# Rotary halves and key scaling of each layer's first step written on VectorE instead of GpSimd

## The chip, the cores and the metric

One core of one Trainium2 chip runs the whole program. The time is the device time of one execution in microseconds (us). It is taken from timed runs; one more execution was recorded by the hardware profiler and gives the rows below. The engines are TensorE (PE in the rows; PEld is its weight load), VectorE (DVE), ScalarE (ACT), GpSimd (POOL) and SyncE (SP).

## What is computed

A two-layer model on 16 sequences of 256 tokens, 128 channels: linear attention, a mixture of experts, a retention block, and last a block of two local-attention layers with feed-forward parts. The change lies in the local attention. Cut to what matters:

```
h = shift_token(x)
q, k, v = split(h @ wqkv)                 # 8 heads of 64
q = l2norm(q) * qs;  k = l2norm(k) * ksc
q = q * cos * scale + rotate_half(q) * sin * scale
k = k * cos / scale + rotate_half(k) * sin / scale
o = local_attention(q, k, v)              # windows of 64, one window back
x = x + o @ wo
```

for 2 layers, each followed by a feed-forward part.

## The kernel before

The attention of a layer (`local_layer`, lines 1977 to 2429) walks over 8 chunks of 512 tokens. A chunk is 4 tiles of 128 tokens. Each engine has a program of its own, written out by hand; semaphores alone order the engines against each other. `steps` (line 2012) calls `step` ten times on each engine: in a step a new chunk is projected (`project`), the chunk before it is attended (`attend`) and the one before that is finished (`finish`). The first step of a layer has `project` alone; the second has `project` and `attend`. So each layer begins with one step in which nothing but the projections of its first chunk runs, until two pairs of heads of that same chunk are attended in its last tile.

What one tile t passes through:

- TensorE: `project_qk` for queries, then for keys (line 2128, three matmuls each). The one for queries waits for `v_sb`, the copy of the values of tile t-1, because it takes that bank.
- ScalarE: `squares` (line 2264) of queries and of keys, the squares for the norms.
- VectorE: `rotate` (line 2354) of queries and of keys, which multiplies the bank by cosines and by sines into `R`; then `lengths` (lines 2361 and 2364), the sums of squares.
- TensorE: `project_v` (line 2137), which waits for both rotations because it takes the bank of the keys; ScalarE copies it out (`keep_values`, line 2290).
- GpSimd: `add_halves` (line 2053, two instructions) adds the cosine and sine parts; then in even tiles `next_low` (lines 1664 and 1666) and in odd ones `mix_values` (lines 2075 and 2076); then `scale_keys` (line 2062), which multiplies the keys by their inverse norms `rn`.
- ScalarE: `norms` (lines 2269 and 2272) gives `rn`. It is called one tile later, as the second piece of work of tile t+1, behind `squares` of its queries.
- TensorE: `turn_keys` (line 2149) and `turn_queries` (line 2158) transpose `R` of tile t, within tile t+1.

VectorE also runs `maxima` (line 2377), the score maxima of two heads in four instructions, twice a tile once attention runs, and `reciprocals` (line 2384). In the first step's last tile it runs `rotate`, `maxima` of pair 0, `lengths`, `maxima` of pair 1.

Below, a layer's tiles are counted from 0: tiles 0 to 3 are its first step, tile 4 is the first tile of its second step. `summed` counts added halves, `normed` scaled keys, `rnorm` inverse norms.

Of the kernel before, what the change touches and what calls it, by code (L numbers as in the profile page):

```python
# [11 lines left out]
ALU = mybir.AluOpType  # L12
# [3 lines left out]
P = 128  # L16
# [19 lines left out]
DEPTH, HEADS, DH, WIN = 2, 8, 64, 64  # L36
# [1930 lines left out]
NTILE = CH // P  # L1967
# [9 lines left out]
def local_layer(k, l, shared):  # L1977
# [4 lines left out]
    nc, ps = k.nc, k.ps  # L1982
    with ExitStack() as big:
# [5 lines left out]
        with ExitStack() as ctx:  # L1989
# [50 lines left out]
            @block.gpsimd  # L2040
            def _(pool):

                def next_low(g, par, part):
                    wait_alone(k, pool, hs_hi, 2 * (g + l) + part + 1)
                    shift_low(k, g, l, par, part)
                    wait_alone(k, pool, shifted, 2 * (g + l) + part + 1)

                def add_halves(g, t):
                    n, i = NTILE * g + t, t % 2
                    halves = R[:, i, :, :, :].rearrange("p q c (h z d) -> p q c h z d", z=2, d=DH // 2)  # L2050
                    wait_alone(k, pool, rotated, 2 * n + 2)
                    for z in range(2):
                        nc.gpsimd.tensor_tensor(halves[:, :, 0, :, z, :], halves[:, :, 0, :, z, :],  # L2053
                                                halves[:, :, 1, :, 1 - z, :], ALU.add).then_inc(summed, 1)

                def scale_keys(c, par, t):
                    n, i = NTILE * c + t, t % 2
                    wait_alone(k, pool, summed, 2 * n + 2)
                    wait_alone(k, pool, rnorm, n + 1)
                    x = R[:, i, 1, 0, :].rearrange("p (h d) -> p h d", d=DH)  # L2060
                    scale = rn[:, par, t, HEADS:2 * HEADS].rearrange("p (h o) -> p h o", o=1)
                    nc.gpsimd.tensor_tensor(x, x, scale.to_broadcast([P, HEADS, DH]), ALU.mult).then_inc(normed, 1)  # L2062

                def scale_weights(c, p):
                    wait_alone(k, pool, rden_r, NPAIR * c + p + 1)
                    x = W[:, p % RING, :].rearrange("p (a b) -> p a b", a=4)
                    scale = rden[:, p % RING, :].rearrange("p (a o) -> p a o", o=1)
                    nc.gpsimd.tensor_tensor(x, x, scale.to_broadcast([P, 4, P]), ALU.mult).then_inc(scaled, 1)  # L2068

                def mix_values(c, par, s):  # L2070
                    need(pool, av_mm, NPAIR * (c - 2) + NB * (s + 1))
                    pool.wait_ge(v_sb, NTILE * c + 2 * s + 2)
                    pool.wait_ge(summed, 2 * (NTILE * c + 2 * s + 2))
                    pool.sem_inc(v_seen, 1)
                    nc.gpsimd.tensor_copy(VM[par][0:DH, s, :, :], VA[par][0:DH, 2 * s + 1, :, :]).then_inc(v_mixed, 1)
                    nc.gpsimd.tensor_copy(VM[par][DH:P, s, :, :], VA[par][DH:P, 2 * s, :, :]).then_inc(v_mixed, 1)
                    wait_alone(k, pool, v_mixed, 2 * (SPC * c + s + 1))

                def step(g, par, project, attend, finish):
                    now = (g, par, project, attend, finish)  # L2080
                    for t in range(NTILE):
                        for lag in (8, 7):
                            sc = staged(*now, 2 * t, lag)
                            if sc:
                                scale_weights(sc[0], sc[2])
                        if project:
                            add_halves(g, t)
                            if t % 2:
                                mix_values(g, par, t // 2)
                            else:  # L2090
                                pool.wait_ge(summed, 2 * (NTILE * g + t + 1))
                                next_low(g + 1, 1 - par, t // 2)
                            scale_keys(g, par, t)
                        elif attend:
                            split_part(t // 2, t % 2)

                done = lambda i: 2 * NX + 3 * DEPTH + 2 * l + i + 1

                def split_part(i, part):
                    n = names[1 + i]  # L2100
                    hi, lo = parts[n]
                    if part == 0:
                        pool.wait_ge(w_in, L * 16 * len(names))
                        nc.gpsimd.tensor_scalar(hi[:], w[n][:], 1.0, None, ALU.mult).then_inc(k.w_hi, 1)
                    else:
                        pool.wait_ge(k.w_hi, done(i))
                        nc.gpsimd.tensor_tensor(lo[:], w[n][:], hi[:].bitcast(F32), ALU.subtract).then_inc(k.w_lo, 1)

                steps(pool, step)
                pool.wait_ge(k.w_lo, done(1))  # L2110
                pool.wait_ge(resid, SPC * (G0 + 2))
                for i in range(2):
                    ffn_shift(k, i, here(G0 + i), ffn_shifted)
                pool.wait_ge(ffn_shifted, 2 * (G0 + 2))
# [228 lines left out]
            def _(dve):  # L2343
# [13 lines left out]
                def lengths(g, t):  # L2357
                    n, i = NTILE * g + t, t % 2
                    dve.wait_ge(squared, 2 * n + 2)
                    need(dve, rnorm, n - 1)  # L2360
                    nc.vector.tensor_reduce(sums[:, i, :, 0:1].rearrange("p h o -> p (h o)"),  # L2361
                                            sq[:].rearrange("p q (h d) -> p (q h) d", d=DH), AX.X, ALU.add).then_inc(sums_r, 1)
                    dve.wait_ge(sums_r, n + 1)
                    nc.vector.tensor_reduce(ss[:, i, :], sums[:, i, :, :], AX.X, ALU.max).then_inc(clipped, 1)

                def maxima(c, par, p):
                    b, s = p % NB, p // NB
                    if b == 0:
                        dve.wait_ge(rnorm, NTILE * c + 2 * s + 2)
                    need(dve, wT_mm, NPAIR * c + p - RING + 1)  # L2370
                    for i in range(2):
                        dve.wait_ge(s_mm, NU * c + 2 * p + i + 1)
                        dve.sem_inc(s_seen, 1)
                        for t in range(2):
                            j, h = 2 * i + t, 2 * b + i
                            cols = slice(t * P, (t + 1) * P)
                            m = nc.vector.tensor_tensor_reduce(W[:, p % RING, j * P:(j + 1) * P], ps[BS[i]][:, cols],  # L2377
                                                               k.const["mask_q"][:, cols], rn[:, par, 2 * s + t, h:h + 1], FAR,
                                                               ALU.add, ALU.min, nm[:, p % RING, j:j + 1])
                        m.then_inc(max_r, 1)  # L2380
# [17 lines left out]
                def step(g, par, project, attend, finish):  # L2398
                    now = (g, par, project, attend, finish)
                    for t in range(NTILE):  # L2400
                        even, odd = 2 * t, 2 * t + 1
                        rc = staged(*now, even, 8)
                        next_rc = staged(*now, even, 7)
                        mx = staged(*now, even, 6)
                        next_mx = staged(*now, odd, 6)
                        ks = staged(*now, odd, 11)
                        next_ks = staged(*now, odd, 10)
                        if project:
                            rotate(g, t)
                        if rc:  # L2410
                            reciprocals(rc[0], rc[2])
                        if mx:
                            maxima(*mx)
                        if next_rc:
                            reciprocals(next_rc[0], next_rc[2])
                        if t == 3 and attend:
                            add_output(g - 1, 0)
                        if t == 1 and finish:
                            add_output(g - 2, 1)
                        if project:  # L2420
                            lengths(g, t)
                        if ks:
                            keep_sums(*ks)
                        if next_ks:
                            keep_sums(*next_ks)
                        if next_mx:
                            maxima(*next_mx)
# [396 lines left out]
```

## Time and profile before

| | |
|---|---|
| median of 3 timed runs | 1371.28 us (1366.42 to 1371.88) |
| profiled execution, its own time | 1358.34 us |
| its span, first to last instruction | 1356.5 us |
| busy: PE, DVE, ACT, POOL | 1170.2, 1035.9, 883.5, 889.6 us |
| first step of layer 1 | from 643 us |
| first step of layer 2 | from 991 us |

The shares over the whole span mix stages with different limits. What matters here are two stretches of some 28 us, each the first step of a layer, and which wait ends last in them.

### The profile page before, as it was taken

Reading aid. Unit: us, or ns where it says so; the run is one execution under the profiler, and the core shown is the slowest. Engines: PE = TensorE matmul, PEld = TensorE weight load, DVE = VectorE, ACT = ScalarE, POOL = GpSimd, SP = SyncE. Lnnn points to the kernel's source line nnn. Section 1 sums busy time; section 2 is a strip of 40 time slices with the busy share of each in tenths; the row PEclk is TensorE's granted clock in tenths of the full one; section 3 lists DMA queues with packets and bytes.
Section 4 is the critical chain, followed back from the end, with each engine's and each line's share of the span. In section 5 each row is a group of like instructions: output and inputs, shape, how many; then the busy total and the mean of one; then the engine's idle time right before and its main releaser. Section 6 shows DMA issues by size and latency. Waiting matters only on the chain. (4 is left out here: it accounts for less than half of the span.)

```text
span 1356.5 us, 26609 instructions
## 1 busy us (share of the span) xinstructions
PE 1170.2 (86%) x7852; PEld 792.3 (58%) x7852; DVE 1035.9 (76%) x2641; ACT 883.5 (65%) x2332; POOL 889.6 (66%) x821
## 2 busy tenths in 40 slices
PE   7689998736889994797799999988979999999897
PEld 4344544414568883342477777774646767677565
DVE  6699999736988883664688888866658888887555
ACT  5545555324545551375699999976549989899564
POOL 0378888176616665414688888886658888788663
PEclk9899999857999997699799999999979999999999
DMA  4520000032302213300000000000000000000002
GB/s 134 211 71 0 1 0 1 3 110 69 121 31 71 71 53 101 114 0 6 20 2 2 1 0 0 0 1 1 1 24 2 2 3 1 1 1 1 1 0 62
DMA packets 35166, 43.99 MB, mean 32 GB/s; under 512 B 5636, under 2 KB 24993, under 8 KB 35056
## 3 DMA queue, kind: packets, MB, share of 16 engines
q1 hardware_dynamic: 30448, 34.27, 7.9%
q0 software_dynamic: 4608, 8.47, 1.9%
q8 instruction: 43, 0.70, 0.2%
q14 instruction: 67, 0.55, 0.1%
HBM read 22.65 MB, written 21.12 MB: 32 GB/s over the span
## 5 line engine op out<-in xcount | busy, mean ns | idle before, releaser
L2354 DVE TENSOR_TENSOR R<-bank,tab 128x1024 f32<-128x1024 f32 x128 | 156.2, 1224 | 67.6 <-ACT sq L2264 66.9
L2298 ACT ACTIVATE W<-W,nm 128x128 f32<-128x128 f32 x512 | 198.2, 393 | 0.4
L2053 POOL TENSOR_TENSOR R<-R 128x512 f32<-128x512 f32 x128 | 161.1, 1280 | 15.6 <-DVE R L2354 15.6
L2377 DVE CUSTOM_DVE_ANT_0 W<-bank,mask_q,rn 128x128 f32<-128x128 f32 x512 | 147.5, 344 | 17.3 <-PE bank L2174 12.6
L2068 POOL TENSOR_TENSOR W<-W,rden 128x512 f32<-128x512 f32 x128 | 132.5, 1040 | 36.8 <-DVE rden L2384 31.6
L1563 POOL DMA_INDIRECT expert_rows<-Yt,xin x80 | 82.5, 1031 | 84.6 <-DVE Yt L1536 63.6
L2298 ACT ACTIVATION_READ_ACCUMULATOR W<-W,nm 128x1 f32 x512 | 98.7, 193 | 0.0
L2282 ACT ACTIVATE QK<-bank 128x512 f32<-128x512 f32 x128 | 74.9, 585 | 35.0 <-PE bank L2149 33.8
L235 POOL DMA_INDIRECT expert_slots<-token_rows,dst x64 | 66.9, 1045 | 38.2 <-issue 29.7
L2199 PE MATMUL bank<-PT,VA 128*64 128x128 f32 (+1 forms) x1024 | 85.4, 260 | 4.0 <-ACT PT L2306 3.1
L2174 PE MATMUL bank<-QK 64*64 64x128 f32 x2048 | 85.7, 282 | 3.3 <-DVE nm L2377 2.8
L2062 POOL TENSOR_TENSOR R<-R,rn 128x512 f32<-128x512 f32 x64 | 66.7, 1042 | 32.2 <-ACT rn L2272 28.1
L2264 ACT ACTIVATE sq<-bank 128x512 f32<-128x512 f32 x128 | 74.5, 582 | 19.4 <-PE bank L2128 16.8
L2306 ACT ACTIVATE PT<-bank 128x512 f32<-128x512 f32 x128 | 74.8, 589 | 6.5 <-PE bank L2184 6.5
L2361 DVE TENSOR_REDUCE sums<-sq 128x16 f32<-128x1024 f32 x64 | 76.8, 1200 | 0.0
L876 DVE TENSOR_TENSOR_SCAN S<-beta,bank 128x512 f32<-128x512 f32 x64 | 76.0, 1209 | 0.6
L2184 PE MATMUL bank<-ident,W 128*128 128x128 f32 x512 | 75.7, 273 | 0.0
L2199 PEld LDWEIGHTS bank<-PT,VA 128*64 128x64 f32 x1024 | 51.8, 137 | 40.7 <-issue 40.5
L2128 PE MATMUL bank<-wqkv_hi,hs_hi 128*128 128x512 f32 x128 | 64.4, 503 | 11.1 <-ACT QK L2282 4.5
L2184 PEld LDWEIGHTS bank<-ident,W 128*128 128x128 f32 x512 | 62.6, 140 | 15.9 <-issue 0.7
L2481 POOL TENSOR_TENSOR Uf_lo<-Uf,Uf_hi 128x512 fp32r<-128x512 f32 (+1 forms) x44 | 56.3, 1289 | 20.2 <-DVE Uf_hi L2658 19.6
L2174 PEld LDWEIGHTS bank<-QK 64*64 64x64 f32 x2048 | 55.1, 133 | 20.8 <-issue 16.8
(372 smaller groups left out, 3554.9 us busy)
## 6 DMA issues: line engine op xcount, KB each, us to landing
expert_slots<-empty SPq DMA_DIRECT2D x8, 650.0 KB, 6.3
xin<-expert_slots SPq DMA_DIRECT2D x7, 650.0 KB
expert_rows<-empty SPq DMA_DIRECT2D x8, 512.0 KB, 6.7
token_rows<-expert_rows SPq DMA_DIRECT2D x16, 256.0 KB, 4.2
expert_raw<-w1e_dram SPq DMA_DIRECT2D x9, 256.0 KB
expert_raw<-w2e_dram SPq DMA_DIRECT2D x9, 256.0 KB
tok<-x_dram SPq DMA_DIRECT2D x8, 256.0 KB, 4.5
out_dram<-tok_out SPq DMA_DIRECT2D x8, 256.0 KB, 2.5
```

The lines of the kernel that those rows point to most:

```text
L876: nc.vector.tensor_tensor_scan(S[i][:], beta[i % 2][:, chunk(c)], ps[BV + i // 2][:], 0.0, ALU.mult, ALU.add).then_inc(s_scan, 1)
L1563: nc.gpsimd.indirect_dma_start(k.ys[:, :], bass.IndirectOffsetOnAxis(ap=ids, axis=0), Yt[:, s % 3, t, :], None, bounds_check=2 * T - 1, oo ...
L2053: nc.gpsimd.tensor_tensor(halves[:, :, 0, :, z, :], halves[:, :, 0, :, z, :], halves[:, :, 1, :, 1 - z, :], ALU.add).then_inc(summed, 1)
L2068: nc.gpsimd.tensor_tensor(x, x, scale.to_broadcast([P, 4, P]), ALU.mult).then_inc(scaled, 1)
L2174: m = nc.tensor.matmul(ps[BS[i]][r:r + WIN, blk // 2 * P:(blk // 2 + 1) * P], QK[par][rows, b, o:o + WIN], keys, start=True, stop=True)
L2184: m = nc.tensor.transpose(ps[BT[p % 2]][:, a * P:(a + 1) * P], W[:, p % RING, a * P:(a + 1) * P], k.const["ident"][:])
L2199: m = nc.tensor.matmul(ps[BO[p % 2]][i * DH:(i + 1) * DH, cols], v[:, 2 * b + i, :], PT[:, p % 2, i * SEQ + cols.start:i * SEQ + cols.stop ...
L2282: nc.scalar.activation(QK[par][:, qk * NB:(qk + 1) * NB, t * P:(t + 1) * P], ps[BX[(t + 1) % 2]][:].rearrange("p (a b) -> p a b", a=NB), A ...
L2298: m = nc.scalar.activation(x, x, ACT.Exp, scale=-1.0, bias=nm[:, p % RING, j:j + 1], accum_out=den[:, p % RING, j:j + 1])
L2354: nc.vector.tensor_tensor(R[:, i, qk, :, :].rearrange("p c (h d) -> p c h d", d=DH), x, y.to_broadcast([P, 2, HEADS, DH]), ALU.mult).then_ ...
L2361: nc.vector.tensor_reduce(sums[:, i, :, 0:1].rearrange("p h o -> p (h o)"), sq[:].rearrange("p q (h d) -> p (q h) d", d=DH), AX.X, ALU.add ...
L2377: m = nc.vector.tensor_tensor_reduce(W[:, p % RING, j * P:(j + 1) * P], ps[BS[i]][:, cols], k.const["mask_q"][:, cols], rn[:, par, 2 * s + ...
```

## The change

In the first step of each layer (`attend` is false) GpSimd no longer runs `add_halves` and `scale_keys`; VectorE runs both, behind `lengths` of the same tile. The other steps are as they were.

```diff
@@ GpSimd, step
                         if project:
-                            add_halves(g, t)
+                            if attend:
+                                add_halves(g, t)
                             if t % 2:
                                 mix_values(g, par, t // 2)
                             else:
                                 pool.wait_ge(summed, 2 * (NTILE * g + t + 1))
                                 next_low(g + 1, 1 - par, t // 2)
-                            scale_keys(g, par, t)
+                            if attend:
+                                scale_keys(g, par, t)
@@ VectorE, new functions
+                def add_halves(g, t):
+                    n, i = NTILE * g + t, t % 2
+                    halves = R[:, i, :, :, :].rearrange("p q c (h z d) -> p q c h z d", z=2, d=DH // 2)
+                    dve.wait_ge(rotated, 2 * n + 2)
+                    for z in range(2):
+                        nc.vector.tensor_tensor(halves[:, :, 0, :, z, :], halves[:, :, 0, :, z, :],
+                                                halves[:, :, 1, :, 1 - z, :], ALU.add).then_inc(summed, 1)
+
+                def scale_keys(c, par, t):
+                    n, i = NTILE * c + t, t % 2
+                    dve.wait_ge(summed, 2 * n + 2)
+                    dve.wait_ge(rnorm, n + 1)
+                    x = R[:, i, 1, 0, :].rearrange("p (h d) -> p h d", d=DH)
+                    scale = rn[:, par, t, HEADS:2 * HEADS].rearrange("p (h o) -> p h o", o=1)
+                    nc.vector.tensor_tensor(x, x, scale.to_broadcast([P, HEADS, DH]), ALU.mult).then_inc(normed, 1)
@@ VectorE, step
                         if project:
                             lengths(g, t)
+                            if not attend:
+                                add_halves(g, t)
+                                scale_keys(g, par, t)
```

VectorE, beginning of a layer's first step, from the rotations of tile 0 to `lengths` of tile 1. Before:

```order
L2354 TENSOR_TENSOR R<-bank,tab 128x1024 x2
L2361 TENSOR_REDUCE sums<-sq 128x16
L2364 TENSOR_REDUCE ss<-sums 128x16
L2354 TENSOR_TENSOR R<-bank,tab 128x1024 x2
L2361 TENSOR_REDUCE sums<-sq 128x16
```

With the change (line numbers are two higher from here on):

```order
L2356 TENSOR_TENSOR R<-bank,tab 128x1024 x2
L2363 TENSOR_REDUCE sums<-sq 128x16
L2366 TENSOR_REDUCE ss<-sums 128x16
L2373 TENSOR_TENSOR R<-R 128x2x8x32 x2
L2382 TENSOR_TENSOR R<-R,rn 128x512
L2356 TENSOR_TENSOR R<-bank,tab 128x1024 x2
L2363 TENSOR_REDUCE sums<-sq 128x16
```

The halves (L2373) and the scaled keys (L2382) of tile 0 now stand ahead of the rotations of tile 1 on VectorE.

VectorE, end of the first step: `lengths` of tile 3, `maxima` of pair 1 (the first of its four instructions shown), and on to tile 4. With the change, buffer numbers kept:

```order
L2363 TENSOR_REDUCE sums0<-sq0 128x16
L2366 TENSOR_REDUCE ss0<-sums0 128x16
L2373 TENSOR_TENSOR R0<-R0 128x2x8x32 x2
L2382 TENSOR_TENSOR R0<-R0,rn0 128x512
L2395 ISA W0,nm0<-bank2,mask_q,rn0 128x128
```

Before, the rows `L2373` and `L2382` were not there: the maxima followed `lengths` at once. Now the scaled keys of tile 3 stand ahead of the maxima of pair 1 and of the rotations of tile 4.

GpSimd, the first two tiles of the first step, as a piece of the difference:

```order
-L2053 TENSOR_TENSOR R<-R 128x2x8x32 x2
-L1664 TENSOR_TENSOR hs_lo<-H,hs_hi 64x512
-L2062 TENSOR_TENSOR R<-R,rn 128x512
-L2053 TENSOR_TENSOR R<-R 128x2x8x32 x2
-L2075 COPY VM<-VA 64x512
-L2076 COPY VM<-VA 64x512
-L2062 TENSOR_TENSOR R<-R,rn 128x512
```
```order
+L1664 TENSOR_TENSOR hs_lo<-H,hs_hi 64x512
+L2075 COPY VM<-VA 64x512
+L2076 COPY VM<-VA 64x512
+L1666 TENSOR_TENSOR hs_lo<-H,hs_hi 64x2x255
+L2075 COPY VM<-VA 64x512
+L2076 COPY VM<-VA 64x512
```

GpSimd keeps the low parts of the next chunk (`hs_lo`) and the mixed values (`VM`); the second fence is the whole of its first step with the change.

## Rows read from the trace of the kernel before

**Rows 1.** The profile's page: the span, and the group of the rotations.

```profile
span 1356.5 us, 26609 instructions
...
L2354 DVE TENSOR_TENSOR R<-bank,tab 128x1024 f32<-128x1024 f32 x128 | 156.2, 1224 | 67.6 <-ACT sq L2264 66.9
```

**Rows 2.** Busy time by stretch: the first step of layer 1.

```profile
core 0: us, PE busy (x) PEld busy (x) DVE busy (x) ACT busy (x) POOL busy (x), PEclk, DMA share, GB/s
643.00:671.00 28.00, 20.94 (x95) 14.03 (x94) 16.31 (x26) 13.61 (x32) 16.74 (x16) 0.67 0.09 29
```

**Rows 3.** Timeline of VectorE, layer 1: start us, us, what, idle before.

```profile
652.10 2.51 DVE L2354 TENSOR_TENSOR R<-bank,tab 128x1024 f32<-128x1024 f32 x2 [3.35 <-ACT sq L2264]
...
658.99 2.36 DVE L2354 TENSOR_TENSOR R<-bank,tab 128x1024 f32<-128x1024 f32 x2 [3.04 <-ACT sq L2264]
...
665.79 2.36 DVE L2354 TENSOR_TENSOR R<-bank,tab 128x1024 f32<-128x1024 f32 x2 [3.10 <-ACT sq L2264]
668.06 0.34 DVE L2377 CUSTOM_DVE_ANT_0 W<-bank,mask_q,rn 128x128 f32<-128x128 f32 x1
...
669.14 1.21 DVE L2361 TENSOR_REDUCE sums<-sq 128x16 f32<-128x1024 f32 x1
...
670.55 0.35 DVE L2377 CUSTOM_DVE_ANT_0 W<-bank,mask_q,rn 128x128 f32<-128x128 f32 x1
...
672.33 2.39 DVE L2354 TENSOR_TENSOR R<-bank,tab 128x1024 f32<-128x1024 f32 x2 [0.39 <-ACT sq L2264]
```

**Rows 4.** Timeline of TensorE: values and queries at tile 0, turned keys and values at tile 3.

```profile
647.45 0.79 PE L2137 MATMUL bank<-wqkv_hi,hs_hi 128*128 128x512 f32 x1 [1.95 <-DVE R L2354]
...
649.78 0.79 PE L2128 MATMUL bank<-wqkv_hi,hs_hi 128*128 128x512 f32 x1 [0.69 <-ACT VA L2290]
...
667.55 0.63 PE L2149 MATMUL bank<-ident,R 128*128 128x128 f32 x4 [1.15 <-POOL R L2062]
668.20 0.50 PE L2137 MATMUL bank<-wqkv_hi,hs_hi 128*128 128x512 f32 x1
```

**Rows 5.** Timeline of ScalarE: inverse norms of tiles 0 to 3, value copies of tiles 0 and 3.

```profile
649.13 0.60 ACT L2290 ACTIVATE VA<-bank 128x512 f32<-128x512 f32 x1 [2.48 <-PE bank L2137]
...
652.20 0.31 ACT L2272 ACTIVATE rn<-ss,lnb 128x16 f32<-128x16 f32 x1
...
659.23 0.31 ACT L2272 ACTIVATE rn<-ss,lnb 128x16 f32<-128x16 f32 x1
...
665.89 0.31 ACT L2272 ACTIVATE rn<-ss,lnb 128x16 f32<-128x16 f32 x1
...
669.20 0.60 ACT L2290 ACTIVATE VA<-bank 128x512 f32<-128x512 f32 x1 [0.38 <-PE bank L2137]
...
672.43 0.31 ACT L2272 ACTIVATE rn<-ss,lnb 128x16 f32<-128x16 f32 x1
```

**Rows 6.** VectorE, all instructions of line 128, both inputs in SBUF: ns min/median/max.

```profile
L128 DVE TENSOR_TENSOR XT<-XT,H x8: 685/686/692, 1345.2 to 1349.5; 128x512 f32<-128x512 f32 x8
```

**Rows 7.** Timeline of GpSimd: the last copy of mixed values in the first step.

```profile
671.62 0.61 POOL L2076 COPY VM<-VA 64x512 f32<-64x512 f32 x1
```

**Rows 8.** Timelines of GpSimd and of VectorE in layer 1's feed-forward part.

```profile
983.25 2.67 POOL L2481 TENSOR_TENSOR Uf_lo<-Uf,Uf_hi 85x512 fp32r<-85x512 f32 x2 [1.82 <-DVE Uf_hi L2658]
...
985.56 1.51 DVE L2669 TENSOR_TENSOR Uf_lo<-Uf,Uf_hi 128x512 fp32r<-128x512 f32 x2
```

**Rows 9.** The waits of 643 to 671 us: us in total, times, longest.

```profile
PE bank L2149 <- POOL R L2062: 4.2, 3, 1.9
```

**Rows 10.** Timelines of VectorE and of ScalarE, layer 2: rotations, inverse norms.

```profile
1000.05 2.50 DVE L2354 TENSOR_TENSOR R<-bank,tab 128x1024 f32<-128x1024 f32 x2 [3.21 <-ACT sq L2264]
...
1020.42 2.39 DVE L2354 TENSOR_TENSOR R<-bank,tab 128x1024 f32<-128x1024 f32 x2 [0.57 <-ACT sq L2264]
...
1000.15 0.31 ACT L2272 ACTIVATE rn<-ss,lnb 128x16 f32<-128x16 f32 x1
...
1020.52 0.31 ACT L2272 ACTIVATE rn<-ss,lnb 128x16 f32<-128x16 f32 x1
```

## The prediction

> **What bounds the kernel now.** I began at the page, found the rotations as VectorE's costliest group, and saw that nearly all of the idle time ahead of them ends with a square on ScalarE [rows 1]. The change acts in two stretches of 28 us, so I read those and not the shares of the span. In the first of them no engine is full: TensorE, the busiest, has 20.94 us of 28, VectorE 16.31, GpSimd 16.74, and the granted clock is 0.67 on average [rows 2]. A stretch in which nobody is full is bound by a chain, and the timelines name it.
>
> The chain of one tile: when both rotations are done, TensorE starts on the values (647.45) because they take the bank of the keys; ScalarE copies them out (649.13 to 649.73); TensorE then projects the queries of the next tile (649.78) [rows 4, 5]; ScalarE squares them, and the rotation of the next tile starts at 652.10 [rows 3]. The rotations start at 652.10, 658.99, 665.79 and 672.33 [rows 3], so a tile takes 6.5 to 6.9 us, and all of it is this circle. GpSimd is beside it: `turn_keys` does wait for its scaled keys, 1.15 us in tile 3, but the values that follow start at 668.20, just when the rotation that they need anyway is over (665.79 + 2.36 = 668.15) [rows 3, 4]. The 4.2 us that TensorE waits for GpSimd's keys in this stretch [rows 9] are spent while VectorE still rotates.
>
> **What the change does, part by part.**
>
> *Work taken off GpSimd.* In each first step two adds and one scaling a tile. Nobody on the chain waits for them, as just shown, so I count no gain. `next_low` and `mix_values` wait for the same `summed` as before and no longer stand behind the adds; their readers come a step later.
>
> *Adds on VectorE.* Two instructions of 128 by 512 a tile with both inputs in SBUF. The nearest row is 0.69 us [rows 6]. Two rotations of 1.224 us take 2.36 together [rows 1, 3], so a follower starts about 0.08 before the end of its forerunner: the pair takes 0.61 + 0.69 = 1.3 us. They stand in VectorE's idle time of 3 us ahead of each rotation [rows 3], less the 1.4 us of `lengths` (669.14 to 670.55). Cost nothing, as long as the scaling behind them waits for something later still, which it does. In tile 3, the fullest, the rotations with pair 0's maxima and `lengths` end at 670.55, the adds would at 671.85, and the norms come at 672.74 [rows 3, 5]: 0.9 us of cover, and over 2 us in the tiles without maxima.
>
> *The scaling on VectorE.* This is the part that costs. The scaling of tile t waits for `rnorm` of tile t, which ScalarE makes only within tile t+1, behind the squares for which the rotation of tile t+1 waits. VectorE runs in order, so these rotations are now queued behind a wait that ends later than their own. Before, the rotations of tiles 1 to 4 started at 652.10, 658.99, 665.79, 672.33 [rows 3]; the inverse norms of tiles 0 to 3 were done at 652.51, 659.54, 666.20, 672.74 (start plus 0.31) [rows 5]. The norms are 0.41, 0.55, 0.41 and 0.41 us later. To each comes the start of the scaling after its release, 0.04 (value copy over at 649.73, queries start at 649.78 [rows 4, 5]), and the scaling itself, 0.61 until the follower starts. So the rotations of tiles 1, 2 and 3 come later by 1.06, 1.20 and 1.06, in all 3.32 us. Each delay is passed on whole, since rotation, values, copy, queries and squares are one circle and the norms hang on the same squares.
>
> *Tile 3 to tile 4.* Here the maxima of pair 1 stand between the scaling and the rotation. Before, they ran from 670.55 in time that VectorE had, with 0.39 us of idle time left ahead of the rotation at 672.33 [rows 3]. Now they too are behind the norms: 0.41 + 0.04 + 0.61 and four maxima, 1.08 (668.06 to 669.14, the ones of pair 0 [rows 3]), is 2.14 us.
>
> Sum of a layer: 3.32 + 2.14 = 5.46 us. In layer 2 the rotations of tiles 1 and 4 start at 1000.05 and 1020.42 and the norms end at 1000.46 and 1020.83 [rows 10], again 0.41 behind, so I take the same. Two layers: 10.9 us.
>
> *GpSimd's copies beside the scaling of tile 3.* Before, the maxima of pair 1 began at 670.55; moved by 3.32, the adds of tile 3 run there from 673.87 to 675.2. GpSimd then starts its two copies of mixed values, which took from about 670.96 to 672.23 [rows 7], and would now be in the second until about 676.6, while the scaling is released at 672.74 + 3.32 + 0.04 = 676.1. Does this matter? In the feed-forward part VectorE started a two-input instruction at 985.56 while a GpSimd one ran until 985.92; two of 0.69 would take 1.30 together, these took 1.51 [rows 6, 8]. The first of them thus ended 0.56 after GpSimd did instead of 0.69 after its own start. For the scaling of tile 3 that gives 676.6 + 0.56 = 677.2 instead of 676.8: 0.35 us a layer, 0.7 for both. Its bounds: 0 if the copies are over by then, 0.6 (a whole copy) if the scaling has to start behind them, so 0 to 1.2 for both layers. The other three scalings meet an idle GpSimd.
>
> The Trainium skill ("SBUF — State Buffer", section "Who interferes with whom") says that a VectorE instruction with two SBUF inputs and a GpSimd instruction that reads SBUF exclude each other, and that the second fully blocks. By that rule the scaling of tile 3 would wait for the copy's end, 0.5 us a layer, and the sum would be 11.9 instead of 11.6. The row of the feed-forward part agrees in kind, with less in size.
>
> *Sum.* 10.9 + 0.7 = 11.6 us. Against the profiled execution, 1358.34 + 11.6 = 1369.9. The timed runs have their median at 1371.28, 0.95% above it; I take the shift as it is: 1371.3 + 11.6 = 1382.9, say 1383.
>
> **The rivals.**
>
> *The delay is partly swallowed.* If in the second step another engine than VectorE led, it would catch up some of the 5.46. For it: ScalarE's next exponentials wait for only half of pair 1's maxima, so ScalarE is later by about 4 us and not 5.5 at that point. Against it: its value copy of tile 4 waits for TensorE, which waits for the rotation of tile 4, and all that follows hangs on that. If only the three simple delays were passed on, 2 x 3.32 = 6.6, the time is 1378; that is the lower case, 10%.
>
> *TensorE's clock stays low for longer.* With tiles of 8 us in place of 6.9 TensorE has more idle time, and the mean granted clock was 0.67 in this step already [rows 2]: between 1.2 and 2.4 GHz. At the lower level the values took 1.68 us from their start to their copy (647.45 to 649.13), in tile 3 at the upper level 1.00 (668.20 to 669.20) [rows 4, 5]. 0.68 us for each of the values and queries of tiles 2, 3 and 4 that would fall to the lower level, of which I count three more a layer: 2 us a layer, so 1387. 15%.
>
> *The relief of GpSimd pays (faster).* TensorE waits 4.2 us a layer for GpSimd's scaled keys [rows 9]. If that were on the chain after all, and VectorE's scaling cost nothing there, up to 8.4 us would go: 1363. It decides from the point at which the scaled keys come earlier than the rotations' end, and the rows show that end to end within 0.05 us (668.15 and 668.20). 3%.
>
> *Nothing to be measured.* The scaling would have to find its norms ready, that is, ScalarE would have to be an instruction ahead; then only the scalings themselves cost, 4 x 0.61 x 2 = 4.9, so 1376, within 0.5% (6.9 us, about what a measurement of this kernel can tell from no change). Against it: the norms are called behind the very squares that release the rotation. 9%.
>
> **How the numbers follow.** My forecast has 63%, with a range of its own from 1380 to 1386: 10.9 to 12.1 for the bounds of the copies, and some 2 us to either side for the spread of the timed runs. The lower case (1378, 10%) straddles the bound at 6.9: half of it counts as same. Together: slower by over 0.5% 63 + 15 + 5 = 83%, same 9 + 5 = 14%, faster 3%. The range that leaves out no more than 2 in 10 takes in the low-clock case and the swallowed one: 1376 to 1389.
>
> **What would show it.** In the changed profile: (1) the adds and the scaling on VectorE at 0.69 us each; (2) the idle time ahead of the scaling ended by ScalarE's `rn`, in all four tiles; (3) the rotations of tiles 1 to 4 later by 1.1, 2.3, 3.3 and 5.5 to 5.9 us than before; (4) no wait of TensorE for GpSimd in the turned keys of the first step; (5) the second steps and all later ones as long as before, so that the whole gap stands by tile 4 of each layer; (6) the scaling of tile 3 longer than the others by 0.3 to 0.5 us. Wrong I would be if the second step came out shorter than before, if the clock moved otherwise, or if a strided add cost much more than the 0.69 of a plain one: beyond the cover of tile 3, which two adds of over 1.1 us would use up, they would push the scaling itself.

## The result

| | before | with the change |
|---|---|---|
| median of 3 timed runs | 1371.28 us | 1387.43 us (1387.08 to 1388.44) |
| ratio, 95% interval | | 1.0115 [1.0089, 1.0140] |
| profiled execution, its own time | 1358.34 us | 1387.43 us |
| its span | 1356.5 us | 1385.6 us |

The change makes the kernel 16.2 us slower by the medians, 1.2%. A later comparison of six timed runs with seventeen of before (e12) gave 1.0119 [1.0093, 1.0145]; its medians are 0.99% apart, inside that interval. Ratios leave out executions over 1.5% above the fastest of their kernel in the same comparison, so those of e1 to e4 rest on three of eleven runs of before and on two to four of their own, and e3's profile is of such an execution, with its excess ahead of layer 1.

The two profiles differ by 29.1 us, and not all of that is the change. The first rotation of layer 1 starts at 661.90 with the change and started at 644.95 before: 16.95 us arise ahead of the first local layer, whose code is the same. They arise in the experts' stage: the retention block behind it starts 17.0 us later as well (570.8 against 553.8). From that rotation to the end it is 723.7 us against 711.55, and these 12.15 us lie behind the change's first instruction. So below I use a local measure, the span minus the start of layer 1's first rotation; e6 shows why that is fair.

The page of the changed kernel, to be read against [rows 1]:

```profile
span 1385.6 us, 26593 instructions
...
L2356 DVE TENSOR_TENSOR R<-bank,tab 128x1024 f32<-128x1024 f32 x128 | 155.8, 1223 | 49.8 <-ACT sq L2266 49.0
```

The idle time ahead of the rotations fell from 67.6 to 49.8 us, the part of it that ended with a square from 66.9 to 49.0. That looks like a gain and is none: the idle time has moved in front of the scaled keys. The waits of 661.9 to 700 us (us in total, times, longest), and the timeline of VectorE there, to be read against [rows 3]:

```profile
DVE R L2382 <- ACT rn L2274: 8.2, 4, 2.7
```
```profile
669.56 0.69 DVE L2382 TENSOR_TENSOR R<-R,rn 128x512 f32<-128x512 f32 x1 [2.67 <-ACT rn L2274]
670.17 2.35 DVE L2356 TENSOR_TENSOR R<-bank,tab 128x1024 f32<-128x1024 f32 x2
...
677.19 0.69 DVE L2382 TENSOR_TENSOR R<-R,rn 128x512 f32<-128x512 f32 x1 [2.13 <-ACT rn L2274]
677.80 2.35 DVE L2356 TENSOR_TENSOR R<-bank,tab 128x1024 f32<-128x1024 f32 x2
...
683.99 0.69 DVE L2382 TENSOR_TENSOR R<-R,rn 128x512 f32<-128x512 f32 x1 [1.29 <-ACT rn L2274]
684.60 2.35 DVE L2356 TENSOR_TENSOR R<-bank,tab 128x1024 f32<-128x1024 f32 x2
...
689.29 1.28 DVE L2373 TENSOR_TENSOR R<-R 128x512 f32<-128x512 f32 x2
692.69 0.69 DVE L2382 TENSOR_TENSOR R<-R,rn 128x512 f32<-128x512 f32 x1 [2.11 <-ACT rn L2274]
...
694.38 2.35 DVE L2356 TENSOR_TENSOR R<-bank,tab 128x1024 f32<-128x1024 f32 x2
```

All four scalings wait for the inverse norms. The rotations of tiles 1 to 3 follow 0.61 us behind the start of one, without an idle time of their own; that of tile 4 follows 1.69 us behind, with the maxima of pair 1 in between. The busy time by tile, from rotation to rotation, first with the change, then before (column PEclk is the granted clock, 0.50 being 1.2 GHz and 1.00 being 2.4 GHz):

```profile
core 0: us, PE busy (x) PEld busy (x) DVE busy (x) ACT busy (x) POOL busy (x), PEclk, DMA share, GB/s
661.90:670.17 8.27, 5.12 (x11) 2.65 (x9) 5.57 (x8) 3.19 (x7) 1.28 (x1) 0.50 0.14 51
670.17:677.80 7.63, 5.15 (x17) 3.40 (x17) 5.47 (x9) 4.15 (x9) 1.22 (x2) 0.70 0.00 0
677.80:684.60 6.80, 4.31 (x33) 2.87 (x33) 5.47 (x9) 3.17 (x7) 1.09 (x1) 1.00 0.00 0
684.60:694.38 9.78, 5.83 (x33) 3.95 (x33) 7.64 (x23) 5.25 (x18) 1.22 (x2) 0.83 0.00 1
694.38:702.49 8.11, 7.49 (x52) 5.36 (x53) 6.05 (x25) 5.68 (x21) 5.34 (x5) 0.58 0.01 3
```
```profile
644.95:652.10 7.15, 4.52 (x11) 2.65 (x9) 3.77 (x5) 2.34 (x5) 3.77 (x3) 0.50 0.15 56
652.10:658.99 6.89, 5.74 (x19) 3.79 (x17) 3.76 (x5) 4.00 (x9) 4.75 (x5) 0.58 0.00 0
658.99:665.79 6.80, 4.90 (x22) 3.59 (x22) 3.67 (x5) 3.42 (x8) 4.63 (x4) 0.75 0.00 1
665.79:672.33 6.54, 4.63 (x49) 3.03 (x49) 6.05 (x21) 4.59 (x16) 4.77 (x5) 1.00 0.00 1
672.33:679.01 6.68, 5.53 (x55) 3.63 (x54) 6.06 (x22) 6.52 (x25) 5.00 (x5) 1.00 0.01 2
```

Tile by tile the change costs 1.12, 0.74, 0.00, 3.24 and 1.43 us, 6.53 by the rotation of tile 5; in layer 2 it is 6.59. After tile 5 nothing more is added. Tile 2 costs nothing here, but its clock is 1.00 with the change and 0.75 before; tile 4, whose own work the change does not touch, costs 1.43, and its clock is 0.58 instead of 1.00. So two things are mixed, waits and clock; e6 and e9 take them apart.

TensorE at the turn from tile 3 to tile 4, to be read against [rows 4]:

```profile
694.61 0.67 PE L2176 MATMUL bank<-QK 64*64 64x128 f32 x16 [2.23 <-DVE nm L2395]
695.65 1.11 PE L2151 MATMUL bank<-ident,R 128*128 128x128 f32 x4 [0.38 <-DVE R L2356]
696.78 0.80 PE L2139 MATMUL bank<-wqkv_hi,hs_hi 128*128 128x512 f32 x1
```

It waits 2.23 us for VectorE's maxima (`nm`), which are behind the scaling, and then runs at the lower level: 0.80 us for the first of the values' matmuls and not the 0.50 of [rows 4]. But this is the second fall of the clock. There is one before it, in tile 3. By stretch of the granted clock:

```profile
688.36:691.77 3.41, 3.41 (x25) 2.65 (x21) 2.18 (x4) 2.60 (x11) 0.85 (x2) 0.50 0.00 0
691.77:695.18 3.41, 1.18 (x19) 0.63 (x17) 2.49 (x10) 2.48 (x11) 0.36 (x1) 1.00 0.00 0
695.18:702.01 6.83, 6.43 (x36) 4.47 (x33) 5.25 (x22) 4.40 (x16) 4.86 (x5) 0.50 0.02 4
```

The granted clock is 0.50, 1.00 and 0.50 in the three. The wait of 2.23 us ends at 694.61. The fall in tile 3 is over by then, so this wait can't be what caused it.

### The profile page after: what moved, and what is told of

Its sections match the earlier page's. It is cut to its first block and busy times, and to the rows that moved or that the text cites. A ratio compares the mean times of both kernels' runs of the same rounds, so it can differ in the third digit from the quotient of the medians.

```text
span 1385.6 us, 26593 instructions
## 1 busy us (share of the span) xinstructions
PE 1180.2 (85%) x7852; PEld 798.2 (58%) x7852; DVE 1048.6 (76%) x2665; ACT 884.9 (64%) x2332; POOL 861.3 (62%) x797
## 5 line engine op out<-in xcount | busy, mean ns | idle before, releaser
L2356 DVE TENSOR_TENSOR R<-bank,tab 128x1024 f32<-128x1024 f32 x128 | 155.8, 1223 | 49.8 <-ACT sq L2266 49.0
L2395 DVE CUSTOM_DVE_ANT_0 W<-bank,mask_q,rn 128x128 f32<-128x128 f32 x512 | 147.1, 343 | 17.1 <-PE bank L2176 12.9
L2053 POOL TENSOR_TENSOR R<-R 128x512 f32<-128x512 f32 x112 | 141.2, 1282 | 0.0
L2062 POOL TENSOR_TENSOR R<-R,rn 128x512 f32<-128x512 f32 x56 | 58.4, 1042 | 25.2 <-ACT rn L2274 20.8
```

Of the source, the lines that this page charges most:

```text
L2356: nc.vector.tensor_tensor(R[:, i, qk, :, :].rearrange("p c (h d) -> p c h d", d=DH), x, y.to_broadcast([P, 2, HEADS, DH]), ALU.mult).then_ ...
```

## The experiments

The theory W: VectorE's rotations are queued behind a wait for the inverse norms. Rival A: VectorE's added work costs, wherever it waits. Theory C, formed on seeing tile 4: what lies above the waits is TensorE's clock. "Local" is the span minus the start of layer 1's first rotation.

### e1, e12: the change again

> The changed kernel once more, in five rounds against the kernel before, to see how much of the 16 us is the change. In the two profiles so far the rotations of tile 5 come 6.5 us later against those of tile 0, in layer 1 and in layer 2, which makes 13; the other 17 us between the two profiles stand ahead of the first layer, in the experts' stage, which the change doesn't touch. If that stage merely varies from run to run, the ratio comes nearer to 1 + 13/1371 = 1.0095 and the time to 1384; if the change has moved it too, the ratio stays at 1.012 or more and the experts' stage of this profile is again some 17 us longer than that of before.

> The changed kernel a third time, in five rounds. From layer 1's first rotation to the end 723 to 726 us as in its two profiles (711.5 and 707.6 for the kernel before); ratio 1.009 to 1.012.

Measured: e1 has 1373.55 us and a ratio of 1.0073 [0.9974, 1.0172]; on that chip the runs of the kernel before went from 1353.97 to 1384.73 us, too wide to tell. e12, as expected: 1387.41 us, 1.0119 [1.0093, 1.0145]. Local 725.6 and 724.9 us, the first profile had 723.7. The first rotation of layer 1 started at 647.68 in e1 and at 660.22 in e12, under the same code, so the experts' stage was not 17 us longer again in e1.

### e6: the kernel before again

> The kernel before, profiled again. If the experts' stage varies from run to run and the layers do not, the time from layer 1's first rotation to the end is 711.5 us within 2 (the spread being TensorE's clock), while the time ahead of it (644.95 in the first profile) may move by 10 us and more.

Measured: local 707.6 us, first rotation at 662.28 (644.95 in the first profile). So the stages ahead move by 17 us between profiles of one program and the layers by 4, twice what I expected. Of the 3.9 us, 2.9 lie in tiles 0 to 2 of the two layers and go with the clock: tile 2 took 5.70 us at a granted clock of 1.00 here, 6.80 at 0.75 in the first profile. The mean of the three changed profiles is 724.7, that of the two of before 709.6: the change costs 15.1 us locally, in agreement with 16.2 and 13.5 between the medians. Single pairs of these profiles lie between 12.2 and 18.0 us apart, so 15.1 is good to some 2 us.

### e2: only the scaling on VectorE

```diff
@@ against the changed kernel, GpSimd
-                            if attend:
-                                add_halves(g, t)
+                            add_halves(g, t)
@@ VectorE
                             if not attend:
-                                add_halves(g, t)
                                 scale_keys(g, par, t)
```

> Only the scaling of the keys goes to VectorE, the adds stay on GpSimd. Theory W (the rotations are queued behind a wait for the inverse norms): same delay as the full change, rotations of tile 5 against tile 0 later by 6.5 us a layer (6 to 7), ratio 1.008 to 1.012. Rival A (VectorE's added work costs, above all the adds): about 1.3 us a tile less, so 2 us a layer or below, ratio under 1.004.

Measured: the rotation of tile 5 comes 6.43 us (layer 1) and 6.62 us (layer 2) later than before, local 725.2, against 724.7 for the changed kernel. The whole of the change's cost is there without the adds: W holds, A is out. The ratio, 1.0051 [0.9871, 1.0232], is too wide to tell.

### e3: only the adds on VectorE

```diff
@@ against the changed kernel, GpSimd
                             if attend:
                                 add_halves(g, t)
+                            elif t:
+                                wait_alone(k, pool, normed, NTILE * g + t)
...
-                            if attend:
-                                scale_keys(g, par, t)
+                            scale_keys(g, par, t)
@@ VectorE
                             if not attend:
                                 add_halves(g, t)
-                                scale_keys(g, par, t)
```

> Only the adds go to VectorE, GpSimd keeps scaling the keys (and waits for its own scaling of the tile before ahead of the next piece of work, since nothing else orders the two). Theory W: the adds lie in VectorE's idle time; only in tile 3 do they push the maxima of pair 1 by 1.3 us, of which 0.4 was idle, so about 0.9 us a layer, ratio 1.000 to 1.003. Rival A (work costs): 1.3 us in each tile, 5 us a layer, ratio 1.007 or more.

Measured: local 710.4 us, 0.8 above the mean of before, which is less than two profiles of one kernel differ by; ratio 0.9961 [0.9835, 1.0087], too wide to tell. Tile 3 takes 6.99 us in both layers at a full clock, 0.45 above the 6.54 of before, the other tiles no more than before at a like clock. I had expected 0.9 for tile 3; the adds cost half of that, 0.9 us in both layers where the whole change costs 15.1.

### e4: inverse norms a tile earlier

```diff
@@ against the changed kernel, ScalarE, step
-                        if rows:
+                        if rows and attend and (t or not isinstance(g, int) or g > G0 + 1):
                             norms(*rows)
...
                         if next_ex:
                             weights(next_ex[0], next_ex[2])
+                        if project and not attend:
+                            norms(g, par, t)
```

> The changed kernel, but in the first step ScalarE makes the inverse norms of tile t at the end of tile t and not within tile t+1. VectorE's work stays what it is with the change, only what the scaling waits for comes earlier. Theory W: no scaling waits for norms behind the squares any more; the delay falls from 6.5 to about 1.3 us a layer (adds and scaling of tile 3, 1.9 us, less the idle time of 0.4 and the norms that ScalarE saves in tile 4), ratio 1.001 to 1.004. Rival A: the delay stays above 4 us a layer, ratio 1.006 or more.

Measured: local 711.4 us, 1.8 above the mean of before and 13.3 below the change, ratio 0.9960 [0.9837, 1.0083], too wide to tell. VectorE does the same work; only what it waits for is earlier. Tile 3 takes 7.79 us in both layers, 1.25 more than before, as expected. This is the clearest of the runs: 13 of 15 us hang on when ScalarE makes four small tiles a layer.

### e5: the scaling between the two rotations

`rotate` also gets `par` and `attend` handed in, which the cut below leaves out.

```diff
@@ against the changed kernel, VectorE
                     for qk in range(2):
+                        if qk and not attend and t:
+                            scale_keys(g, par, t - 1)
+                        if qk and isinstance(g, int) and g == G0 + 1 and t == 0:
+                            scale_keys(G0, 1 - par, NTILE - 1)
...
                             if not attend:
                                 add_halves(g, t)
-                                scale_keys(g, par, t)
```

> The changed kernel with the scaling of tile t moved between the two rotations of tile t+1 (queries, scaling, keys); it then finds its norms ready, or nearly. Measured from layer 1's first rotation to the end of the profile, where the kernel before has 711.5 us. Theory W (what cost was the wait for the norms, and the scaling's 0.61 us on the chain): the wait goes and the 0.61 us a tile stay on the chain of the keys' rotation, plus 0.6 for the adds ahead of the maxima in tile 3: 3.1 us a layer at most, 6 in all, against 12 to 14 with the change. Rival B (VectorE has so much in the first step that the place does not matter): 12 or more.

Measured: local 714.4 us, 4.8 above the mean of before, 10.3 below the change. That is within the 6 us expected. The norms are ready when the scaling comes up: none of the four waits. At a full clock tile 2 takes 6.29 us, 0.59 above the 5.70 of e6, which is the scaling alone; tile 3 takes 1.05 more than before and layer 1's tile 4, in which the keys of tile 3 are scaled, 0.44. Layer 2's tile 4 took 8.26 us at a clock of 0.79, though nobody waited for norms there.

### e7, e8, e9: TensorE's idle time filled

The kernel before (e7) and the changed one (e8) with additional matmuls, whose results nobody reads; e9 adds three more at the end of the first step and eight in tile 4.

```diff
+                def fill(par, count):
+                    for _ in range(count):
+                        nc.tensor.matmul(ps[BT[0]][:], hs[0][par][:, 0:P], k.lw[l]["wqkv"][0][:, 0:INNER], start=True, stop=True)
@@ step, ahead of turn_keys
+                        if project and not attend:
+                            fill(par, 4)
@@ step, behind turn_queries
+                        if project and not attend and t < 3:
+                            fill(par, 1)
@@ e9: there fill(par, 1 if t < 3 else 3), and ahead of scores
+                        if isinstance(g, int) and g == G0 + 1 and t == 0:
+                            fill(par, 8)
```

> The kernel before with idle TensorE filled in each layer's first step: four matmuls of 128 by 512 into an unused bank ahead of the turned keys, one behind the turned queries, per tile. The first step had a granted clock of 0.67. Theory C (the excess of 6.5 over the 5.5 that waits alone give is TensorE's clock): with the clock up, values and queries take 1.0 instead of 1.7 us each, so layer 2 gains 2 to 4 us and layer 1 up to 4, 711.5 down to 704 to 708. Rival: the fillers themselves stand in the way and it gets slower.

> The changed kernel with the same fillers. Theory C: the difference to the filled kernel before is that of the waits alone, 10.9 us (10 to 12) from layer 1's first rotation to the end, and the delays of tiles 1 to 4 are 1.06, 1.1, 1.06 and 2.14 us in both layers. Rival: the difference stays at 13 or above, so the excess is not the clock.

> The changed kernel with the fillers of before and with eleven more at the end of the first step: three behind the turned queries of tile 3 and eight in tile 4 ahead of the scores of pair 2, where TensorE waits 2.28 us for the maxima of pair 1 and then runs at the lower level for some 7 us. The delay of tile 5 against tile 0 was 8.4 us in layer 1 and 6.9 in layer 2 more than in the filled kernel before. Theory C (what lies above the waits alone, 5.46 a layer, is the lower level that follows TensorE's new wait): with the clock kept up through tiles 4 and 5, layer 2's delay at tile 5 falls to 5.4 to 6.0. Rival: it stays at 6.9, and the order of the work in tile 4 costs by itself.

Measured: e7, as expected, has a ratio of 0.9956 [0.9934, 0.9977] to the kernel before and local 704.2 us; e8 1.0057 [1.0039, 1.0074] and 719.2. The difference is 15.0 us and not the 10.9 that I expected: e8 misses, and by its totals alone its rival holds (13 or above, the excess isn't the clock). The granted clock shows that the fillers of e8 did not do what they were put in for. In layer 1 tile 1 took 8.19 us at a clock of 0.79, 2.50 more than in e7. The busy time by tile in layer 2; first e7, then e8:

```profile
1003.72:1009.41 5.69, 3.70 (x15) 2.42 (x14) 3.66 (x4) 2.46 (x5) 3.11 (x3) 1.00 0.28 104
1009.41:1015.10 5.69, 4.59 (x24) 3.25 (x23) 3.67 (x4) 3.89 (x9) 4.69 (x5) 1.00 0.00 0
1015.10:1020.94 5.84, 4.61 (x27) 2.96 (x25) 3.67 (x4) 3.43 (x8) 5.12 (x6) 1.00 0.00 0
1020.94:1027.48 6.54, 5.75 (x53) 3.71 (x53) 5.93 (x21) 4.59 (x16) 5.14 (x6) 1.00 0.00 0
1027.48:1034.17 6.69, 5.54 (x55) 3.65 (x54) 6.09 (x23) 6.53 (x25) 5.02 (x6) 1.00 0.01 2
```
```profile
1011.60:1018.42 6.82, 4.66 (x18) 2.85 (x17) 5.47 (x7) 3.52 (x8) 1.28 (x1) 1.00 0.25 95
1018.42:1025.36 6.94, 4.85 (x22) 3.37 (x22) 5.47 (x9) 3.71 (x8) 1.22 (x2) 1.00 0.00 0
1025.36:1032.16 6.80, 5.04 (x36) 3.52 (x37) 5.46 (x8) 3.17 (x7) 1.09 (x1) 1.00 0.00 0
1032.16:1041.25 9.09, 5.16 (x36) 2.91 (x34) 7.99 (x23) 5.13 (x18) 1.22 (x2) 0.97 0.00 0
1041.25:1048.91 7.66, 7.43 (x52) 5.39 (x53) 6.05 (x24) 5.68 (x21) 4.89 (x5) 0.59 0.01 3
```

In tiles 0 to 2 both have the full clock and the change costs 1.13, 1.25 and 0.96, in all 3.34 us. Tile 3 costs 2.55. Tile 4 costs 0.97, at a clock of 0.59: the fillers did not reach it. In e9 they do. Its last two tiles of layer 1:

```profile
681.56:690.65 9.09, 7.52 (x47) 4.97 (x45) 7.63 (x23) 5.12 (x18) 1.22 (x2) 1.00 0.01 3
690.65:697.19 6.54, 5.14 (x52) 3.61 (x53) 6.04 (x25) 5.47 (x21) 3.84 (x4) 1.00 0.00 1
```

Tile 4 falls to 6.54 us in both layers at a clock of 1.00, below the 6.69 of e7. So its excess was the clock, and the rival (the order of work in tile 4) is out. In layer 1 the whole delay against e7 is 5.85 us, of which 0.35 are the fillers themselves: they delay the norms of tile 3, and the scaling starts 7.40 us behind its tile's first rotation instead of 7.05 in e8, where it then lost 0.34 to a copy of GpSimd. In layer 2 it is 7.02 and not the 5.4 to 6.0 expected: there tile 1 took 8.20 us at a mean clock of 0.79 in spite of the fillers, 1.26 more than the same tile of e8. Why it fell just there I can't tell. Locally e9 has 718.6 us, still 14.4 above e7: 5.85 and 7.02 stand by the rotation of tile 5, and the rest, 1.5, behind the first steps, most of it behind layer 2's last rotation. So the fillers show where the clock's part lies, tile by tile; no pair of runs shows a total without it.

### e10: the maxima ahead of the scaling

```diff
@@ against the changed kernel, VectorE
                             if not attend:
                                 add_halves(g, t)
-                                scale_keys(g, par, t)
+                                if t < NTILE - 1:
+                                    scale_keys(g, par, t)
...
                             maxima(*next_mx)
+                        if project and not attend and t == NTILE - 1:
+                            scale_keys(g, par, t)
```

> The changed kernel, but in tile 3 the scaling of the keys stands behind the maxima of pair 1 and not ahead of them. Theory W+C: the maxima no longer wait for the norms, TensorE's wait of 2.2 us in tile 4 goes and with it the fall of the clock; tile 4 comes 1.06 later instead of 2.14 or more, so that a layer is delayed by 3.5 to 5 us instead of 6.5, and from layer 1's first rotation to the end 8 to 10 us instead of 12 to 14. Rival: nothing changes (12 or more), because the rotation waits for the same norms.

Measured: local 722.5 us, 12.9 above the mean of before, ratio 1.0115 [1.0079, 1.0150]. The expectation misses. TensorE no longer waits for the maxima, but in layer 1 it now waits 1.29 and 0.47 us for the rotations of tile 4. The rotation of tile 4 comes 3.9 to 4.9 us late instead of the 5.1 to 6.6 of the changed profiles; but the clock of tile 3 is 0.80 in both layers and that of tile 4 is 0.78 and 0.63 all the same. So the wait for the maxima isn't what lowers the clock, or not alone; for tile 3 the order of events in the first changed profile already ruled it out. That part of C falls: filling TensorE's idle time removes the loss (e9), removing this one wait does not.

### e11: early norms and fillers

The edits of e4 and of e8 together.

> Early norms and fillers together, as a version that might beat both kernels. By theory W the change costs nothing with early norms, and by theory C the fillers give 7 us from layer 1's first rotation to the end: 704 us there, ratio 0.995, level with the filled kernel before. If GpSimd's relief is worth anything once nothing waits for the norms, it shows here: 702 or below.

Measured: local 708.2 us, ratio 0.9986 [0.9965, 1.0007]; e7, without the change, has 704.2 and 0.9956. I had expected 704 and 0.995, so this misses too. The 4 us between them are 1.25 us of tile 3 in each layer, 0.5 of clock in layer 1's tile 4 (0.76), and the rest outside of the first steps. GpSimd's relief shows no gain (702 or below) even when nobody waits long for the norms. The version that beats both kernels is e7: GpSimd keeps the work, TensorE's gaps are filled.

## Why the prediction held, and where it was off

The time, 1387.4 us, lies inside the range of 1376 to 1389, on the forecast side, 4.5 us above the forecast itself, outside the forecast's own 1380 to 1386 and level with the low-clock rival's 1387, which had been given 15%. The 11.6 us of the sum would be a ratio of 1.0085, just below both measured intervals.

- **Nothing gained on GpSimd's side: right.** From 661.9 to 700 us TensorE's turned keys no longer wait for GpSimd; all four of their waits, 6.4 us, end with VectorE's `R`. e11 has no gain either.
- **Adds in idle time: right.** 1.28 us for two, 1.3 forecast. In the whole change they cost nothing, as forecast: the scaling behind them in tile 3 waits 2.11 us more, and e2 without them is as slow. Alone, with no scaling behind them, they cost 0.45 in tile 3 (e3).
- **The scaling queued behind the norms: right, mechanism and size.** 0.69 us each, all ended by `rn` (2.67, 2.13, 1.29, 2.11 us). Forecast 3.32 us for tiles 0 to 2 (1.06, 1.20, 1.06); e8 against e7 at full clock 3.34 (1.13, 1.25, 0.96), so that the sum agrees better than its parts, by some luck. Without fillers the same three tiles cost 1.86 us in layer 1 and 3.11 in layer 2 of the first profile, since their clocks differ from those of before. Shown by e2 (scaling alone costs it all), e4 and e5 (earlier norms or a later place remove it).
- **Tile 3 to 4: right in e8.** Forecast 2.14 and 0.35 for the copies, 2.49; e8 against e7 2.55. In the first changed profile, at a clock of 0.83, it is 3.24.
- **GpSimd's copies: right in size where it happens.** In e8 and in e12's layer 1 the scaling of tile 3 starts in GpSimd's second copy and takes 0.34 longer. The timelines of VectorE and GpSimd in e12:

```profile
691.72 1.03 DVE L2382 TENSOR_TENSOR R<-R,rn 128x512 f32<-128x512 f32 x1 [1.07 <-ACT rn L2274]
```
```profile
691.59 0.61 POOL L2076 COPY VM<-VA 64x512 f32<-64x512 f32 x1
```

  It ends at 692.75, 0.55 behind the copy's end, where the prediction had worked out 0.56 from the feed-forward row [rows 8]. In the first changed profile it is 0.69 and the term nothing: the copies were over at 692.13 and the scaling started at 692.69, behind matmuls at the lower level. The Trainium skill ("SBUF — State Buffer", "Who interferes with whom") has a VectorE instruction with two SBUF inputs and a GpSimd instruction that reads SBUF contend for an exclusive lock. If the scaling had done all of its work behind the copy, it would have ended at 692.20 + 0.69 = 692.89. The row agrees in kind and shows 0.14 less, so it seems that part of the instruction passes while it waits.
- **The clock: the term that was missing.** The waits, copies included, make 3.34 + 2.55 = 5.9 us a layer by e8 and e7, 11.8 in all, where the prediction had 11.6. Measured locally is 15.1. The other 3.3 us I put down to TensorE's clock, by subtraction and within the 2 us of the local measure; shown is that tile 4's excess goes when its clock is kept up (e9), and that tile 3's 3.24 falls to 2.55 with it (e8). The prediction had this as a rival at 15% and priced it at 2 us a layer, from the right rows; the step that failed is that it was kept out of the sum, at nothing; its sign ("if the clock moved otherwise") came true. The rival had placed it in tiles 2 to 4; it lies in tiles 3 and 4 above all: there every changed profile has 0.82 to 0.97 and 0.57 to 0.77 where those of before have 1.00 and 1.00. In tiles 0 to 2 the clock goes both ways from profile to profile, also without the change (e6).
- **Later steps as long as before: right from tile 5 on, wrong for tile 4.** From the rotation of tile 5 to that of tile 31 the first profile has 205.03 us against 205.05 before in layer 1, and 210.09 against 210.18 in layer 2. But the gap does not stand by tile 4, as the prediction's signs had it: tile 4 adds 1.43 us in layer 1, by the clock.

In short, the chain of waits was right in mechanism and size. That the time fell into the range was not owed to it alone: the upper part of the range had been opened for the low clock.

What stays open is what exactly lets the granted clock fall in tile 3. The wait that I blamed comes after that fall, and in e10, which removed the wait, the clock fell still. The change also makes TensorE wait longer for what it turns: in layer 1 the turned keys in tiles 1 to 3 wait 1.78, 2.46 and 1.77 us where they waited 1.15, 1.90 and 1.15. No run isolates that.

## What to carry to other kernels

An instruction moved to an idle engine brings its waits along. Ask what stands behind it in that engine's order, and whether its input is made before or after the event that releases this follower; 0.4 us of difference, with the instruction itself, cost 1.1 us in each turn of the circle, and nearly 2 us of work in a gap of 3 cost nothing (tiles 0 to 2 of e4). When a delay goes into a circle that TensorE is part of, price its clock into the sum and not into a rival. And where one stage of a program varies by more than the effect, measure from a landmark behind it.

## What the runs showed of the hardware that was not expected

- Adding matmuls made a kernel faster: with nineteen fillers in each first step the granted clock was 1.00 in all of its tiles but the very first (0.82), and 5.4 us were gone (704.2 against 709.6 locally), ratio 0.9956 [0.9934, 0.9977]. Tiles 0 to 2 took 5.7 to 5.8 us each; without fillers they took 5.7 to 7.2.
- A VectorE instruction with both inputs in SBUF that started during a GpSimd instruction ended 0.55 us behind it, against its own 0.69 undisturbed; in e4 it so took 1.57 us (start 650.59, GpSimd until 651.61), which cost nothing there: the rotation behind it waited another 0.25 us for a square. It goes the other way too: in e4 a GpSimd copy started at 671.13 during a scaling, ended 0.47 us behind it and took 0.99 us instead of 0.61.
- The stages ahead of the local layers ended anywhere from 640.14 to 672.70 us in the fourteen profiles of almost the same program (by the start of layer 1's first rotation), while the local part behind them reproduced within 4 us for the same kernel.
